# A graph layer on one core: VectorE's rounding remainder of the forward product taken two joins earlier, a load moved behind the spread of the sums, and the last step reordered

## Reference, cut to what matters

```python
h = maximum(layernorm(x), 0)                       # x: (16, 512, 128), per batch 512 nodes x 128 features
A_fwd  = [adj, adj, shifted]                       # adj: (16, 512, 512), shifted: roll of the identity
A_list = A_fwd + [transpose(a) for a in A_fwd] + [eye]
HW  = einsum('bnf,rfo->rbno', h, W[:, :F]) + einsum('rd,rdo->ro', W_edges, W[:, F:])[:, None, None, :]
AHW = einsum('rbnm,rbmo->rbno', A, HW)             # 7 relations
return x + max(AHW, axis=0) + b
```

## Time and profile before

| | |
|---|---|
| Median of three runs | 229.85 us (228.3 to 231.33) |
| The profiled execution | 230.3 us, of which its span is 228.5 us |
| PE busy | 214.1 us (94%) |
| PEld, DVE, ACT, POOL busy | 173.4, 182.0, 185.9, 162.8 us |
| DMA | 38.71 MB, mean 169 GB/s |
| Granted TensorE clock | 0.999 of full speed |

### The profile page before, as it was taken

The page is one execution under the profiler, slowest core; times in us unless marked ns, Lnnn a source line. Parts: engine busy times, 40 slices in busy tenths (PEclk is TensorE's granted clock), DMA queues, the critical chain, the costliest instruction groups (busy, mean ns, idle before and its releaser), DMA issues.

```text
span 228.5 us, 4959 instructions
## 1 busy us (share of the span) xinstructions
PE 214.1 (94%) x1069; PEld 173.4 (76%) x1069; DVE 182.0 (80%) x389; ACT 185.9 (81%) x468; POOL 162.8 (71%) x178
## 2 busy tenths in 40 slices
PE   7888998998999999999999999999999999999960
PEld 5667686886878888878888888878888787887740
DVE  4886797894978889697978889697978979676564
ACT  3968997987988888897988888898888889895350
POOL 2560799688595977969596986969596996969120
PEclk9999999999999999999999999999999999999999
DMA  6949868669566768676786967766776965062723
GB/s 213 307 81 279 181 163 246 150 133 267 115 218 131 240 146 198 188 160 217 129 224 139 244 147 172 209 150 210 142 224 147 243 155 142 13 108 83 161 51 50
DMA packets 91152, 38.71 MB, mean 169 GB/s; under 512 B 71575, under 2 KB 80903, under 8 KB 91143
## 3 DMA queue, kind: packets, MB, share of 16 engines
q1 hardware_dynamic: 90055, 38.48, 67.2%
q10 hardware_dynamic: 1088, 0.13, 0.4%
HBM read 34.33 MB, written 4.26 MB: 169 GB/s over the span
## 4 chain that ended last, share of the span: by engine, by line
POOL 50%; issue 31%; DMA 6%; DVE 3%; SPq 3%; PE 3%; POOLq 1%; ACT 1%; ACTq 0%; DVEq 0%
POOL a_lo L306 21%; POOL h_lo L314 8%; POOL o_sb L328 8%; POOL rstd L298 6%; POOL xb_sb L321 5%; DMA a_sb<-in_adj 4%; DMA sum_all<-sums_dram 2%; POOL var_eps L295 1%; POOL neg_mean L296 1%; DVE best L591 1%; POOLq L154 1%; SPq L207 1%; SPq L202 1%; PE at_ps L736 1%; DVE best L588 1%
## 5 line engine op out<-in xcount | busy, mean ns | idle before, releaser
L306 POOL TENSOR_TENSOR a_lo<-a_sb,a_hi 128x512 fp32r<-128x512 f32 x62 | 79.1, 1297 | 39.9 <-ACT a_hi L382 39.9
L591 DVE TENSOR_TENSOR best<-rel_ps,best 128x512 f32<-128x512 f32 x62 | 42.2, 681 | 15.3 <-PE rel_ps L758 14.7
L430 ACT ACTIVATE rel_ps<-sum_all,c_col 128x512 f32<-128x512 f32 (+1 forms) x63 | 41.8, 680 | 8.7 <-DMA sum_all<-sums_dram 6.0
L562 DVE TENSOR_TENSOR at_lo<-at_ps,at_hi 128x512 fp32r<-128x512 f32 x62 | 41.2, 684 | 5.0 <-ACT at_hi L390 4.4
L390 ACT ACTIVATE at_hi<-at_ps 128x512 fp32r<-128x512 f32 x62 | 36.3, 590 | 7.0 <-PE at_ps L736 6.8
L382 ACT ACTIVATE a_hi<-a_sb 128x512 fp32r<-128x512 f32 x64 | 39.4, 622 | 2.8 <-DMA a_sb<-in_adj 2.8
L588 DVE SCALAR_TENSOR_TENSOR best<-rel_ps,c_col,best 128x512 f32<-128x512 f32 x32 | 24.0, 750 | 12.3 <-PE rel_ps L758 10.7
L736 PEld LDWEIGHTS at_ps<-ident,a_sb 128*128 128x128 f32 x240 | 28.0, 141 | 4.9 <-issue 0.8
L736 PE MATMUL at_ps<-ident,a_sb 128*128 128x128 f32 x240 | 31.3, 273 | 0.4 <-DMA a_sb<-in_adj 0.4
L756 PE MATMUL fwd_ps<-at_hi,h_hi 128*128 128x512 f32 x64 | 26.5, 414 | 1.1 <-issue 0.7
L756 PE MATMUL bwd_ps<-a_hi,h_hi 128*128 128x512 f32 x64 | 26.6, 416 | 0.8 <-POOL a_lo L306 0.5
(11 more groups left out here) (102 smaller groups left out, 447.8 us busy)
## 6 DMA issues: line engine op xcount, KB each, us to landing
a_sb<-in_adj SPq DMA_DIRECT2D x64, 256.0 KB, 3.4
sum_all<-sums_dram SPq DMA_DIRECT2D x16, 512.0 KB, 4.4
x_sb<-in_x SPq DMA_DIRECT2D x16, 256.0 KB, 4.4
xp_sb<-in_x SPq DMA_DIRECT2D x64, 64.0 KB, 2.0
out<-o_sb SPq DMA_DIRECT2D x60, 64.0 KB, 2.0
w_sb<-in_L_gnn_W SPq DMA_DIRECT2D x1, 448.0 KB, 5.8
sums_dram<-sum_rows SPq DMA_DIRECT2D x16, 4.0 KB
bias_sb<-in_L_gnn_b SPq DMA_DIRECT2D x4, 64.0 KB, 2.1
```

The lines of the kernel that those rows point to most:

```text
L306: pool.tensor_tensor(a_lo[q][:, j, :], a_sb[q][:, j, :], a_hi[q][:, j, :].bitcast(fp32), ALU.subtract).then_inc(a_lo_ready[j], 1)
L430: act.activation(to[:, cols], sum_all[q][:, 0 if r in FWD else 1, cols], ACT.Copy, scale=c_col[:, r:r + 1]).then_inc(after_it, 1)
L562: dve.tensor_tensor(at_lo[q][:, i, :], at_bank(b, i)[:], at_hi[q][:, i, :].bitcast(fp32), ALU.subtract).then_inc(at_lo_ready[i], 1)
L591: dve.tensor_tensor(best[q][:], held[:], best[q][:], ALU.max).then_inc(joined[r], 1)
```

## The change

Four things. VectorE's `split_fwd` stands ahead of the joins of BWD[1] and EYE[2] in every step of `step`. SP's `load_xp` stands behind the spread in `spread_sums`, in every step but that of batch 0, where it was there already. In the step of b = 15 SP does `spread_sums` first, ahead of the store; ScalarE does `round_fwd` ahead of the fill of BWD[1], VectorE `split_fwd` ahead of the join of BWD[0] and `turn_best` ahead of the join of EYE[2]. In the tail ScalarE's fill of BWD[0] stands ahead of `round_bwd`, VectorE transposes half 0 between the two joins of halves, and GpSimd in place of VectorE makes the sum of half 0.

```diff
             def spread_sums(k, q):
                 sp.dma_start(sums_dram[q][:, :], sum_rows[q][:]).then_inc(sums_stored[q], 16)
                 if is_batch(b, 0):
                     load_by_blocks(bias_sb, bias, bias_loaded)
-                else:
-                    load_xp(k, q)
                 sp.wait_ge(sums_stored[q], 16 * (k + 1))
...
             def step(k, q, more, stored=True):
-                first = is_batch(2 * k + q, 0)
-                if first:
+                sums_first = is_batch(2 * k + q, 0) or is_batch(2 * k + q, B - 1)
+                if sums_first:
                     spread_sums(k, q)
                 if more:
                     reload_x(k, q)
                     reload_a(k, q)
                 if stored:
                     store(k - 1, q)
-                if first:
-                    load_xp(k, q)
-                else:
+                if not sums_first:
                     spread_sums(k, q)
+                load_xp(k, q)
...
             finish(PAIRS - 1, 0)
+            pool.wait_ge(half_turned[0], 1)
+            pool.wait_ge(xb_ready, B)
+            pool.wait_ge(out_stored[1], G * 16 * (PAIRS - 1))
+            pool.tensor_tensor(o_sb[1][:, 0:HALF], turned[1][:, 0:HALF], xb_sb[1][:, 0:HALF],
+                               ALU.add).then_inc(half_out_ready[0], 1)
...
                 if left:
                     round_at(*ahead, 0)
                     take_sums(k, q)
+                else:
+                    round_fwd(k, q)
                 act.wait_ge(joined[FWD[1]], b)
                 fill(*prev, BWD[1], rel_ps[BANK[BWD[1]]], filled[BWD[1]])
...
-                else:
-                    round_fwd(k, q)
...
             fill(k, q, FWD[1], rel_ps[BANK[FWD[1]]], filled[FWD[1]])
-            round_bwd(k, q)
             act.wait_ge(fwd_lo_ready, B)
             fill(k, q, BWD[0], fwd_ps, filled[BWD[0]])
+            round_bwd(k, q)
...
                 join(*prev, FWD[1])
                 if left:
                     split_at(*ahead, 0)
+                else:
+                    split_fwd(k, q)
...
                 if left > 1:
                     mean_and_variance(q)
+                if left:
+                    split_fwd(k, q)
                 join(*prev, BWD[1])
                 if left:
                     split_ht(*ahead)
+                else:
+                    turn_best(*prev)
                 join(k, q, EYE[2])
-                split_fwd(k, q)
-                turn_best(*prev)
+                if left:
+                    turn_best(*prev)
...
+            dve.wait_ge(out_ready, B - 2)
             for half, (held, done, count) in enumerate(...):
                 cols = slice(half * HALF, (half + 1) * HALF)
                 dve.wait_ge(done, count)
                 dve.tensor_tensor(best[q][:, cols], held[:, cols], best[q][:, cols], ALU.max).then_inc(half_joined, 1)
+                dve.wait_ge(half_joined, half + 1)
+                dve.transpose(turned[q][:, cols], best[q][:, cols]).then_inc(half_turned[half], 1)
+            cols = slice(HALF, N)
+            dve.wait_ge(half_turned[1], 1)
             dve.wait_ge(xb_ready, B)
             dve.wait_ge(out_stored[1], G * 16 * (PAIRS - 1))
-            for half, (joined_, count) in enumerate(((half_joined, 1), (joined[BWD[1]], B))):
-                (wait, transpose and sum of each half)
+            dve.tensor_tensor(o_sb[q][:, cols], turned[q][:, cols], xb_sb[q][:, cols], ALU.add).then_inc(half_out_ready[1], 1)
```

More of the change, by code:

```diff
@@ L145, in gnn_layer @@
         best_turned, out_ready = sem("best_turned"), sem("out_ready")
-        half_filled, half_done, half_joined, half_turned, half_out_ready, half_stored = (
-            sem(s) for s in ("half_filled", "half_done", "half_joined", "half_turned", "half_out_ready", "half_stored"))
+        half_filled, half_done, half_joined, half_stored = (
+            sem(s) for s in ("half_filled", "half_done", "half_joined", "half_stored"))
+        half_turned, half_out_ready = pair(sem, "half_turned"), pair(sem, "half_out_ready")
         def wait(eng, semaphore, count):
@@ L186, in store_half @@
             cols = slice(half * HALF, (half + 1) * HALF)
-            queue.wait_ge(half_out_ready, half + 1)
+            queue.wait_ge(half_out_ready[half], 1)
             for g in blocks:
@@ L707, in _ @@
             dve.wait_ge(joined[BWD[0]], B)
-            for half, (held, done, count, after_it) in enumerate(((rel_ps[BANK[EYE[2]]], half_done, 1, half_joined),
-                                                                  (bwd_ps, rel_done[BWD[1]], B, joined[BWD[1]]))):
+            dve.wait_ge(out_ready, B - 2)
+            for half, (held, done, count) in enumerate(((rel_ps[BANK[EYE[2]]], half_done, 1),
+                                                        (bwd_ps, rel_done[BWD[1]], B))):
                 cols = slice(half * HALF, (half + 1) * HALF)
                 dve.wait_ge(done, count)
-                dve.tensor_tensor(best[q][:, cols], held[:, cols], best[q][:, cols], ALU.max).then_inc(after_it, 1)
+                dve.tensor_tensor(best[q][:, cols], held[:, cols], best[q][:, cols], ALU.max).then_inc(half_joined, 1)
+                dve.wait_ge(half_joined, half + 1)
+                dve.transpose(turned[q][:, cols], best[q][:, cols]).then_inc(half_turned[half], 1)
+            cols = slice(HALF, N)
+            dve.wait_ge(half_turned[1], 1)
             dve.wait_ge(xb_ready, B)
             dve.wait_ge(out_stored[1], G * 16 * (PAIRS - 1))
-            for half, (joined_, count) in enumerate(((half_joined, 1), (joined[BWD[1]], B))):
[L716 to L721, removed]
+            dve.tensor_tensor(o_sb[q][:, cols], turned[q][:, cols], xb_sb[q][:, cols], ALU.add).then_inc(half_out_ready[1], 1)
         @block.tensor
```

## The result

The changed kernel took 223.44 us (median of 4 runs, 222.94 to 223.7) against 229.7 us for the kernel before: ratio 0.972, 95% interval 0.966 to 0.979. Timed again beside other kernels it stood at 0.966 (0.962 to 0.971). The profiled execution took 223.7 us with a span of 221.7 us.

A forecast was written before the change was run, and what follows sets the result against it. TensorE, busy 94% of the span, was taken as the bound, so only its waits, start and tail count. 0.86 + 0.27 + 1.25 + 12 x 0.27 = 5.6 plus 2.1 in the tail: 7.7 off 230.3, 222.6 us; range 220.6 to 226.6.

The forecast's parts named there:

- Who holds the 0.25 us: Start of steps b = 2 to 15: VectorE's `fwd_lo` releases TensorE's late first `fwd` load, 0.18 us after it ends.
- rival A: Step starts: the 0.25 us is a fixed cost and stays though `fwd_lo` is early; 226.3 us, chance 0.10.
- What the gap costs: Step starts, turns to second pass: 0.27 us a step from turn and pass spacing; lower bound 0.13 (0.25 - 0.12).
- Cover on VectorE, GpSimd and SP: Work pushed back by the reordering, such as joins, `ht_lo`, x by blocks: costs nothing; blocks of adj move 0 to 0.3 us.
- Spread: Spread of sums ahead of x by blocks: out about 2 us earlier, covering b = 3's 1.37 us fill wait: -1.25 us.
- Edits 1 and 2: `fwd_lo` two joins earlier, 0.27 us a step; x by blocks behind the spread, 1.25 us; b = 2 jointly 0.86 of 1.2.
- Last step and tail: Step b = 15 and tail: earlier spread and new orders bring the end 2.1 us earlier, 1.15 as the bound.
- the 0.7: Tail: 0.7 us spare before POOL's lateness would decide whether the tail's gain is given back.
- rival B: Tail given back: x by blocks, last in SP's queue, or POOL's sum is late; 224.1 us, chance 0.12.
- A rule against it: Tail: POOL's half 0 sum held by VectorE as in rounding of h, 0.95 us later, tail gives 1.15, not 2.1.
- Rival C: SP's queue: x by blocks issues slowly behind each spread, some 2 us a step; slower, 246 us, chance 0.04.
- Rival D: Another wait right behind `fwd_lo` in each step and varying spread landing; only 1 to 3 us come, 228, chance 0.06.

The follow-up runs named there:

- the control: The changed kernel itself, unaltered, timed again on the same chip as later variants: 222.9 us, ratio 0.966 to the kernel before.
- The one-join kernel: Changed kernel with `fwd_lo` ahead of the join of EYE[2] only, behind that of BWD[1] and `ht_lo`: 223.41 us, ratio 0.969.
- edits 3 and 4 alone: Kernel before with only the last step, tail and GpSimd's sum as changed, middle steps as before: 228.79 us, ratio 0.991.
- Edit 1 alone: Kernel before with only `split_fwd` moved ahead of the joins of BWD[1] and EYE[2]: 227.71 us against 230.99, ratio 0.985.
- edit 2 alone: Kernel before with only x by blocks (`load_xp`) behind the spread, no other order of the last step: 228.35 us, ratio 0.987.

## Why the prediction was right

The forecast was 222.6 us; 223.44 was measured. It took 7.7 us off a profiled run of 230.3; the medians fell by 6.3 us here and by 7.9 beside the control (230.76 to 222.9), and the pieces of the profile by 7.86.

- **Who holds the 0.25 us.** Right, and shown from both sides: with `fwd_lo` earlier the idle time goes in every step, with it one instruction later each step grows by 0.60 us, with the same lag of 0.18 us between VectorE's end and the load. The label "issue" was no evidence for a fixed cost (rival A, 226.3 us).
- **What the gap costs.** 0.27 us from the spacing of turns and passes was right; the idle time shown ahead of the load is 0.25, and the lower bound of 0.13 was too careful: the idle time behind turns cost all of itself. Behind passes it cost less, 1.21 us for 1.37 (a step of 14.19 us for one of 12.98), where the forecast had 1.25.
- **Cover on VectorE, GpSimd and SP.** Right in the middle steps: the joins and `ht_lo` came later and no load waited for them. The blocks of adj moved by more than the 0 to 0.3 us of the forecast (the first was issued 0.17 us behind the step's start, now 0.5 to 0.9 from b = 5 on and 2.8 in b = 2 and 3), also without a wait. In b = 2 the sums were not written 0.1 us earlier but 1.04 later, and the two early fills are still late by 0.24 and 0.30 us. The one-join kernel shows that less of a lead would have done, all but at b = 2.
- **Spread.** The gain by the start of b = 4, 2.72 us, was forecast at 0.86 + 0.27 + 1.25 + 0.27 = 2.65. That these agree to 0.1 us is in part luck: counted from the profile of edits 3 and 4 alone, whose steps up to b = 14 are those of the kernel before, the gain is 1.86. The completion of the sums' write was mis-sized: I took 2.1 us and held it to be not under 1.7; it is 1.60 in most steps and 1.22 in the last, but 2.69 in b = 3 and 2.6 in b = 1 (32.24 to 34.87), where four blocks of adj had just been issued. The sentence that the earlier spread keeps the fills' margin in the later steps holds up: without it one or two of eleven fills are late, by 0.3 to 1.0 us.
- **Edits 1 and 2 need each other.** I priced that only for b = 2 and 3. Alone they bring the start of b = 15 forward by 2.93 and 1.41 us, together by 5.76: 1.4 us more than their sum. 1.0 us of it lies ahead of b = 4, the rest is the two late fills. The profiles of each program up to b = 15 lie up to 0.9 us apart, so by the pairs that they allow the 1.4 may be 1.1 to 3.4, but it is not nothing. Edit 1 alone brings TensorE earlier to a spread that is not there yet; edit 2 alone has only the early waits to take away, since no fill waited in the later steps.
- **Last step and tail.** 2.1 forecast, 2.06 measured to the first half store and 2.10 to the end. By the forecast's own rows GpSimd would be free at 219.9 for 221.7, 1.8 us ahead of need, and SP's stores done 0.7 ahead (221.8 for 222.5); it was 2.08 and 0.85. So the 0.7 was SP's margin and not GpSimd's, and rival B was wrong. The size of its sum (0.75 taken, 0.72 measured) was right. But the credit was placed wrongly in one point, since half 0's sum on VectorE ends the kernel at the same time: the gain is that of the rest, the earlier spread and the new orders on ScalarE and VectorE. Edit 2 alone, which sends the last spread 0.8 us earlier, gave 0.84 of it; how the remaining 1.2 us divides was not tested.
- **A rule against it.** The size of its price was misread. VectorE's rounding of h met GpSimd in both steps of the earlier trace rows; alone it takes 0.43 us (at 18.28 in the profile before), so the longer one lost 1.12 us and not 0.95. Nothing like it was seen: GpSimd's sum took 0.72.
- **Rival C**, SP's queue: not seen. With edit 2, x by blocks took 1.9 us to issue in every step from b = 3 to 13, 2.84 at most in b = 2 and 2.9 in the last step, and no step grew by it. The slower stores in b = 2, named above, are the nearest thing to it. **Rival D**, another wait right behind `fwd_lo`: none; the steps take the 12.7 us that the passes and turns make by the forecast's own sum.
- **What the forecast left out** is the start-up, 1.06 us longer in this profile than in before's. The changed kernel itself had 18.74 and 17.79 us; a single pair of profiles can carry that much, and the times of a few runs too.

## What to carry to other kernels

When an idle gap has no named releaser, compare the lag to each candidate's end where that end is out of line with the others: here one odd step out of 14 settled it ahead of any run, and the lag is the same 0.18 us in all 14. Removing the first waiter exposes a transfer that was just in time, so send that transfer earlier in the same change, and judge the two together. With an unrelated start-up that varies by more than the effect, compare pieces of the profiles from a common event on.

## What the runs showed of the hardware

- From the issue of the write of 4 KB of sums to DRAM to the issue of the spread that waits for it, SP took 1.22 us in the last step, where no block of adj is loaded any more, 1.60 in a middle step and 2.6 right behind four blocks of adj; the median landing of x by blocks went from 2.0 to 3.6 us when it was issued behind the 512 KB spread, while the spread's own went from 4.4 to 4.1.
- The rounding of h takes 0.43 us alone and 1.55 us or 0.60 in turn before. Both times an add of GpSimd was running when it started, and both times it ended 0.28 to 0.29 us behind that add's end; in the second case GpSimd's next add took 1.46 us instead of 1.28:

```profile
107.52 1.28 POOL L321 TENSOR_TENSOR xb_sb<-xp_sb,bias_sb 128x512 f32<-128x512 f32 x1
...
119.39 1.29 POOL L328 TENSOR_TENSOR o_sb<-turned,xb_sb 128x512 f32<-128x512 f32 x1
...
120.63 1.46 POOL L321 TENSOR_TENSOR xb_sb<-xp_sb,bias_sb 128x512 f32<-128x512 f32 x1
```

  In the changed kernel, where VectorE starts it ahead of GpSimd's add of x by blocks, it took 0.61 to 0.77 us in the ten steps from 79 to 195 us and that add 1.46 to 1.49. This agrees with the exclusion that the Trainium skill, "SBUF — State Buffer", Who interferes with whom, states: the later one waits.
- The runs of the kernel before lie wider (229.02 to 232.45 us in 10 runs beside the control) than those of the changed one (222.08 to 223.5 in 6). The landing of its spreads took 3.8 to 5.1 us, and its early fills waited for it; that this is the cause was not tested.
